# Ternary weights of a fused cross-attention and feed-forward kernel: the 0/1 mask products on TensorE and their PSUM copies replaced by rounding on VectorE, a sign on ScalarE and transposing DMAs

## The reference

```python
x = x + _L0_xattn_ref(_layernorm(x), ctx_1024, ctx_1024, Wq, Wk, Wv, Wo, lam, g)   # 16 heads x 2 softmaxes, d 32, 154 keys
x = x + _L0_ffn_ref(_layernorm(x), ln1_g, ln1_b, w1, b1, ln2_g, ln2_b, w2, b2)

def ternary_quant(w):
    scale = 1.0 / jnp.clip(jnp.mean(jnp.abs(w)), 1e-05)
    wq = jnp.clip(jnp.round(w * scale), -1.0, 1.0) / scale
    return w + jax.lax.stop_gradient(wq - w)

h = layer_norm(x, ln1_g, ln1_b)
h = jnp.einsum('bsd,hd->bsh', h, ternary_quant(w1)) + b1      # w1: 2048 x 512
h = jax.nn.gelu(h, approximate=False)
h = layer_norm(h, ln2_g, ln2_b)
out = jnp.einsum('bsh,dh->bsd', h, ternary_quant(w2)) + b2    # w2: 512 x 2048
```

## Time and profile before

| | us |
|---|---|
| median of 3 runs (2387.71 to 2390.44) | 2389.39 |
| the profiled execution | 2389.21 |
| its span in the profile | 2387.2 |
| busy: PE | 2280.3 |
| busy: DVE | 1673.4 |
| busy: ACT | 1380.1 |
| busy: POOL | 988.1 |

### The profile page before, as it was taken

The page is one execution under the profiler, slowest core; times in us unless marked ns, Lnnn a source line. Parts: engine busy times, 40 slices in busy tenths (PEclk is TensorE's granted clock), DMA queues, the critical chain, the costliest instruction groups (busy, mean ns, idle before and its releaser), DMA issues.

```text
span 2387.2 us, 35788 instructions
## 1 busy us (share of the span) xinstructions
PE 2280.3 (96%) x13791; PEld 1086.3 (46%) x13791; DVE 1673.4 (70%) x2659; ACT 1380.1 (58%) x2001; POOL 988.1 (41%) x807
## 2 busy tenths in 40 slices
PE   8679999999999999999999999999999999999978
PEld 5344535445353544535354454535445453544433
DVE  4677758586776868678686867868676776857663
ACT  3335655566575656657565655656555565665544
POOL 0101625436172534617153452716345271624417
PEclk9779999999999999999999999999999999999989
DMA  7412103030210303021130302112040211202000
GB/s 264 120 29 63 27 24 84 15 88 21 77 33 24 84 15 89 20 67 27 37 86 15 93 15 67 29 50 58 15 108 15 67 28 61 46 24 67 15 23 18
DMA packets 105661, 125.88 MB, mean 53 GB/s; under 512 B 22512, under 2 KB 74284, under 8 KB 104980
## 3 DMA queue, kind: packets, MB, share of 16 engines
q1 hardware_dynamic: 105492, 123.60, 18.5%
HBM read 51.80 MB, written 20.36 MB: 30 GB/s over the span
## 4 chain that ended last, share of the span: by engine, by line
PE 78%; DVE 11%; SPq 4%; ACT 3%; issue 2%; DMA 1%; POOL 1%; POOLq 0%; ACTq 0%; DVEq 0%
PE ps L1443 16%; PE ps L1465 9%; PE ps L1455 9%; PE ps L1286 6%; PE ps L1287 5%; PE ps L1288 5%; PE ps L1341 5%; PE ps L1388 5%; PE ps L1366 4%; PE ps L1395 4%; DVE attn_raw L1013 2%; SPq L456 2%; DVE arena L1074 2%; DVE arena L975 2%; PE ps L1371 2%
## 5 line engine op out<-in xcount | busy, mean ns | idle before, releaser
L566 POOL TENSOR_TENSOR attn_raw<-attn_raw 128x512 f32<-128x512 f32 x448 | 579.3, 1312 | 153.2 <-ACT attn_raw L723 145.9
L1443 PE MATMUL ps<-rows,w1T 128*128 128x512 f16 x2048 | 486.5, 381 | 6.6 <-DVE rows L1069 6.6
L975 DVE TENSOR_REDUCE arena<-ps 128x3 f32<-128x462 f32 (+1 forms) x704 | 412.8, 617 | 105.4 <-PE ps L1341 104.3
L532 POOL TENSOR_TENSOR q<-q 128x512 f16<-128x512 f32 x128 | 152.6, 1198 | 681.1 <-ACT q L669 679.9
L718 ACT ACTIVATE attn_raw<-ps,vec_cols,wstep 128x512 f32<-128x512 f32 x256 | 198.5, 775 | 215.4 <-PE ps L1443 212.9
L1074 DVE SCALAR_TENSOR_TENSOR arena<-attn_raw,vec_cols,arena 128x512 f16<-128x512 f32 x256 | 232.0, 906 | 87.0 <-ACT arena L721 85.2
L1443 PEld LDWEIGHTS ps<-rows,w1T 128*128 128x128 f16 x2048 | 193.6, 98 | 199.7 <-DVE rows L1069 10.8
L1465 PE MATMUL ps<-w2T,arena 128*128 128x512 f16 x1088 | 271.2, 379 | 0.0
L689 ACT ACTIVATE arena<-ps 128x1024 f32<-128x1024 f32 x128 | 131.6, 1028 | 228.3 <-PE ps L1366 228.3
L995 DVE SCALAR_TENSOR_TENSOR p<-arena,p 128x512 f16<-128x512 f32 x128 | 88.1, 688 | 236.7 <-ACT p L693 236.7
L1341 PE MATMUL ps<-k_att,stack_raw 96*128 96x154 f16 x2048 | 221.9, 233 | 27.5 <-DVE arena L975 25.5
(11 more groups left out here) (185 smaller groups left out, 3482.0 us busy)
## 6 DMA issues: line engine op xcount, KB each, us to landing
stack_raw<-q SPq DMA_DIRECT2D x768, 64.0 KB, 2.0
arena<-in_x SPq DMA_DIRECT2D x64, 256.0 KB, 2.6
out<-arena SPq DMA_DIRECT2D x64, 256.0 KB, 2.0
arena<-in_x SPq DMA_DIRECT2D x15, 1024.0 KB, 6.3
arena<-in_L_ffn_w SPq DMA_DIRECT2D x7, 1024.0 KB, 10.0
stack_raw<-in_L_xattn_Wq SPq DMA_DIRECT2D x8, 256.0 KB, 5.8
k_att<-k_store SPq DMA_DIRECT2D x4, 490.0 KB
k_store<-attn_raw SPq DMA_DIRECT2D x12, 160.0 KB
```

The source lines that it names most:

```text
L566: ins = pool.tensor_tensor(acc[:, e, :], acc[:, e, :], src[:, j % NG, :], ALU.add)
L975: dve.tensor_reduce(negmax[:, tt, u0:u1], ps[:, row_bank(c, tb), 0:(u1 - u0) * S].rearrange("p (u s) -> p u s", s=S), AX.X, ALU.max, negat ...
L1443: ins = pe.matmul(ps[:, B_H + j % 2, :], w1T[:, k, j * P:(j + 1) * P], rows16[:, e, k, :], start=(k == 0 and e == 0), stop=(k == KD - 1 an ...
```

## The change

For each of the 32 tiles:

- DVE adds 1.5 x 2^23 to w * scale, in place and in f32, which rounds it to a whole number (one instruction in place of two).
- ACT takes the sign of the result less that number, and writes it in f16 to one of 16 buffers (w1) or 8 (w2): `ternary_sign`, in place of the copy from PSUM. At the ninth tile of w2 it waits until the first eight have been transposed.
- SP issues a DMA that transposes the tile on its way from this buffer to `w1T` or `w2T` (`transpose_ternary`).
- PE's eight matmuls are gone, and with them its waits for masks and copies.

What waited for the copies now waits for the DMAs: the bias product and ACT's first copy of block 0 for all of w1, `h_transposes(0)` for all of w2, and SP itself ahead of `load_x_res(0)`, since those loads overwrite the buffers of w2's signs.

```diff
-PE_PROLOGUE = tokens("x0 q0 q1 a0 q2 t0 t1 t2 q3 t3 t4 t5 q4 t6 t7 m0 q5 t8 t9 m1 q6 t10 m2 t11 q7 m3 t12 m4 t13 m5 t14 "
-                     "m6 t15 m7 m8 m9 m10 b0 x1 n0")
+PE_PROLOGUE = tokens("x0 q0 q1 a0 q2 q3 q4 m0 q5 m1 q6 m2 q7 m3 m4 m5 m6 m7 m8 m9 m10 b0 x1 n0")
+STACKS_AT = {3: 1, 8: 2, 12: 3}
+X_IN1_AT = 6
...
-        signs_late = x_res_raw.bitcast(F16).rearrange("p (n e t) -> p n e t", n=4, e=2)
+        signs_late = x_res_raw.bitcast(F16).rearrange("p (n t) -> p n t", n=8)
...
+            def transpose_ternary(n):
+                dst, landed = ternary_out(n)
+                sp.wait_ge(s_sign, n + 1)
+                sp.dma_start_transpose(dst, sign_tile(n)).then_inc(landed, 16)
...
                 if i == 0:
+                    for n in range(11):
+                        transpose_ternary(JH + n)
                     for p in range(QATT // 2):
                         stack_queries(1, p, 0)
-                    sp.wait_ge(s_ternT, NTERN)
+                    for n in range(11, JH):
+                        transpose_ternary(JH + n)
+                    sp.wait_ge(s_tern[1], 16 * 8)
+                    sp.wait_ge(s_tern[2], 16 * 8)
                     for tt in range(TT):
                         load_x_res(0, tt)
...
-            for p in range(QM // 2):
-                if p == 2:
-                    sp.wait_ge(s_sign, 4)
+            stack_queries(0, 0, None)
+            for n in range(JH):
+                if n in STACKS_AT:
+                    stack_queries(0, STACKS_AT[n], None)
+                if n == X_IN1_AT:
                     load_x_in(1)
-                stack_queries(0, p, None)
+                transpose_ternary(n)
...
-            def ternary_copy(n):
-                act.wait_ge(s_ternT, n + 1)
-                dst, src = ternary_out(n)
-                act.copy(dst, src).then_inc(s_ternC, 1)
+            def ternary_sign(n):
+                src, _ = natural(n)
+                act.wait_ge(s_round, n + 1)
...
+                elif n == JH + 8:
+                    act.wait_ge(s_tern[1], 16 * 8)
+                act.activation(sign_tile(n), src, ACT.Sign, bias=rounder[:, 0:1]).then_inc(s_sign, 1)
...
-                dve.tensor_scalar(pair[:, 0, :], src, wscale[:, w:w + 1], 0.5, ALU.mult, ALU.is_gt)
-                dve.tensor_scalar(pair[:, 1, :], src, wscale[:, w:w + 1], -0.5, ALU.mult, ALU.is_lt).then_inc(s_sign, 1)
+                dve.tensor_scalar(src, src, wscale[:, w:w + 1], ROUNDER, ALU.mult, ALU.add).then_inc(s_round, 1)
...
-                for k in range(KD):
-                    cols = slice(k * P, (k + 1) * P)
-                    pe.matmul(ps[:, bank, cols], pair[:, 0, cols], ident16[:], start=True, stop=False)
-                    ins = pe.matmul(ps[:, bank, cols], pair[:, 1, cols], nident16[:], start=False, stop=True)
-                ins.then_inc(s_ternT, 1)
```

More of the change, by code:

```diff
@@ L87 @@
                "v7 w14 a3 w15")
-SIGNS_AHEAD = 3
+ROUNDED_AHEAD = 3
+ROUNDER = 1.5 * 2.0 ** 23
+STACKS_AT = {3: 1, 8: 2, 12: 3}
+X_IN1_AT = 6
 W1_CUTS, W2_PIECES = (0, 4, 8, 10, 14, 16), 4
@@ L245, in build @@
         negmaxT = sq_acc[0:2 * UNITS, 0:TB // 2].bitcast(F16)
-        signs = attn_raw[:, 0:8 * TB].bitcast(F16).rearrange("p (n e t) -> p n e t", n=8, e=2)
+        signs = attn_raw[:, 0:8 * TB].bitcast(F16).rearrange("p (n t) -> p n t", n=16)
         k16 = attn_raw[:, 0:KV * BATCH * SPAD // 2].bitcast(F16).rearrange(
@@ L369, in natural, with sign_tile @@
             return gg_raw[:, r * HID + q * D:r * HID + (q + 1) * D], 1
-        def sign_pair(n):
-            return signs[:, (n + 4) % 8] if n < JH else signs_late[:, n % 4]
+        def sign_tile(n):
+            return signs[:, (n + 8) % 16] if n < JH else signs_late[:, n % 8]
         block = es.enter_context(nc.Block())
@@ L894, in ternary @@
                 src, w = natural(n)
-                pair = sign_pair(n)
-                if n in (2, 4):
-                    for half in range(2):
-                        dve.wait_ge(s_vst[half], 16 * (n // 2))
-                if 8 <= n < JH:
-                    dve.wait_ge(s_ternT, n - 7)
-                elif n >= JH + 4:
-                    dve.wait_ge(s_ternT, n - 3)
-                dve.tensor_scalar(pair[:, 0, :], src, wscale[:, w:w + 1], 0.5, ALU.mult, ALU.is_gt)
-                dve.tensor_scalar(pair[:, 1, :], src, wscale[:, w:w + 1], -0.5, ALU.mult, ALU.is_lt).then_inc(s_sign, 1)
+                dve.tensor_scalar(src, src, wscale[:, w:w + 1], ROUNDER, ALU.mult, ALU.add).then_inc(s_round, 1)
             def bias_vector():
@@ L1114, in iteration @@
                 if i == 0:
-                    for n in range(SIGNS_AHEAD):
+                    for n in range(ROUNDED_AHEAD):
                         ternary(JH + n)
@@ L1123, in iteration @@
                         attn_lo(i, n)
-                    elif what == "w" and n + SIGNS_AHEAD < JH:
-                        ternary(JH + n + SIGNS_AHEAD)
+                    elif what == "w" and n + ROUNDED_AHEAD < JH:
+                        ternary(JH + n + ROUNDED_AHEAD)
                     elif what == "g" and i:
@@ L1485, in iteration @@
                         scores(i, n)
-                    elif what == "w":
-                        if queries_done > 1:
-                            wait(pe, s_q32, 1, QM, queries_done)
-                        ternary(JH + n)
-                        tiles_done = n + 1
                     elif what == "v":
@@ L1504, in iteration @@
                     elif what == "q" and ahead:
-                        if i == 0 and n:
-                            pe.wait_ge(s_ternC, JH + tiles_done)
                         queries(i + 1, n)
-                        queries_done = n + 1
                 for tt in range(TT):
@@ L1543, in _ @@
             for what, n in PE_PROLOGUE:
-                if what == "t":
-                    ternary(n)
-                elif what == "x":
+                if what == "x":
                     if n:
```

45 lines of the change are left out of this document (21 added, 24 removed).

## The result

| | us |
|---|---|
| kernel before, same chip, median of 9 runs (2387.71 to 2392.47) | 2390.07 |
| changed kernel, median of 9 runs (2392.98 to 2398.53) | 2396.69 |
| ratio, with its 95% interval | 1.0027 [1.0018, 1.0035] |
| profiled execution of the changed kernel | 2396.69 (span 2394.9) |

What follows compares the result with a forecast made beforehand. The prediction took SP's queue order, not TensorE's share, to bound the prologue's end and block 0; prologue 1.8, block 0 5.5 and clock 1.0 us on 2389.21 gave 2397.6, predicted as 2398 us, range 2386 to 2432.

Steps and rivals of the forecast that it cites:

- +8.3: Whole kernel: prologue 1.8, block 0 5.5 and clock 1.0 us added to the profiled execution's 2389.21 us.
- every link of block 0: Transposing DMAs delay residual loads and x on SP's queue; VectorE waits, TensorE idles some 10 us, its clock falls.
- T: Time one transposing DMA holds SP's queue: taken as 1.6 us, range 0.64 to 3.6.
- Prologue, +1.8: Fourth pair of queries starts at 137.8 instead of 136.03 us, behind twelve transposing DMAs; end of prologue 1.8 us later.
- The bound of -4.5 for a small T: Prologue: at most 4.5 us gained, where the last pair waits for its queries again.
- Block 0, +5.5: Residual loads start at 224.2 instead of 218.69 us behind five transposing DMAs; x and the feed-forward half 5.5 us late.
- 3 us off the pairs: Block 0: TensorE's saving ahead of the fourth query product lets the second pair leave SP at 214.8, not 217.8 us.
- The clock, +1: After block 0's stall TensorE's matmuls take twice 0.21 us until 2.4 GHz is granted again: 1 us.
- About 6 us by its last tiles: Block 0: what the attention half gains as a whole by its last tiles, about 6 us.
- The crossbar is the bound: Rival, chance 0.20: T over 2.4 us, ScalarE may stall too in block 0; 2427 us at 3.1, about 2440 at 3.6.
- the transposing DMAs are cheap: Rival, chance 0.20: T up to 0.9 us; prologue gains 4.5, block 0 loses 2.6, clock 1; 2388 us, no change.
- TensorE's time comes back: Rival, chance 0.08: T at most 0.9 us, block 0's attention half returns TensorE's 7.1 and VectorE's 4 us; 2383 us.

Runs made afterwards that it cites:

- run 1: Changed kernel with block 0's load of x for block 2 issued ahead of the last five transposing DMAs; 2391.92 us, 1.0009 of the kernel before.
- run 2: Changed kernel with w2's signs written in place, residual loads at block 0's start and x ahead of the last five transposing DMAs; 2384.19 us, 0.9976.
- Run 3: Changed kernel with four more transposing DMAs, into a spare tile, ahead of the prologue's fourth pair of queries; 2401.02 us, 1.0046 of the kernel before.
- run 5: Changed kernel with the prologue's fourth pair of queries behind ten transposing DMAs instead of twelve; 2395.66 us, 1.0026 of the kernel before.
- run 4: Changed kernel with 44 matmuls of 512 columns added on TensorE in block 0's stall; 2392.10 us, 1.0006 of the kernel before.
- run 8: Changed kernel with 44 matmuls of one column added on TensorE in block 0's stall; 2395.04 us, 1.0021 of the kernel before.
- run 6: run 2 with the prologue's fourth pair of queries behind ten transposing DMAs instead of twelve; 2384.71 us, 0.9979 of the kernel before.
- run 9: run 6 with one 512-column matmul into an unused bank ahead of the wait for w1's last transposing DMA; 2385.31 us, 0.9977.
- run 10: run 6 with 71 filler matmuls of 512 columns in TensorE's waits through the end of the prologue; 2381.73 us, 0.9971 of the kernel before.
- run 7: w1 made as in the changed kernel, w2 by masks, mask products and copies as in the kernel before; 2391.26 us, 1.0005.
- run 11: run 2 with 44 one-column matmuls added on TensorE in the prologue, at its wait for the third pair of queries; 2381.70 us, 0.9972.

## Why the prediction came out

**Forecast 2398, measured 2396.69.** The sum against the profiled execution was +8.3 and came out at +7.5 (2396.69 against 2389.21). Its mechanism was right in every link of block 0, the main one proved by runs 1 and 2. Its terms were less good than the sum, which came so close by luck: the prologue was forecast 2.2 us too high, and the clock and what lies behind the row transposes together 2 us too low (1.0 and 0.9).

**T.** Taken at 1.6, it is 1.30 us, the value of twice a 64 KB DMA, which the prediction had named as the middle. The rows of the key stores, to which I went because a transposition scatters, were the wrong neighbour. The last lands 2.5 us after its issue begins, 1.2 beyond its end, where I took 1.4.

**Prologue, +1.8.** Measured -0.4. With T = 1.30 the prediction's slope (12 us per us of T) gives -1.8. The rest is one transposing DMA of the second group of three that held the queue 1.71 us instead of 1.27 (its sign had been ready for 11 us) and one of the next two that held it 1.52, the gaps of 0.04 to 0.05 us between groups, a load of x of 0.59 instead of 0.52, and a first pair of 8.2 instead of 7.65, less a start 0.3 us sooner. Run 3 confirms the slope; run 5 shows that two DMAs further down it flattens, since w1's own landing ends the wait. The bound of -4.5 for a small T was too generous: the last low half of the queries came at 133.6 instead of 136.0, 2.4 us sooner.

**Block 0, +5.5.** The loads of the residual came 6.6 us later, from two errors that cancel in part. I took 3 us off the pairs that stand ahead. They began 1.3 us sooner (197.70 against 198.98) and ended 0.4 us sooner (217.42 against 217.80), because one of their 24 DMAs held the queue 1.52 us, where before the longest took 0.64 (duration in ns, least, median and most):

```profile
L460 SPq DMA_DIRECT2D stack_raw<-q x24: 586/597/1519, 197.7 to 216.8; - x24
```

Against that, five transposing DMAs took 6.5 instead of 8.0 us. The load of x then was 5.7 us later (227.16), since the four loads ahead of it were issued in 1.78 instead of 2.71 us, and it landed 0.8 us faster (6.70 against 7.5). That makes the +4.84 on VectorE. Its wait was 11.5 us and not about 9, since the attention half had ended 5 us sooner.

**The clock, +1.** This term was sized at half: 2.0 by the trace, 2.3 by runs 4 and 8. I had the mechanism and no row for how long the low clock lasts; it lasted 6 us (236.2 to 242.3), all of them under matmuls.

**Savings.** Mask products: TensorE is busy 8.4 us less in all, where the pace of the starts gave 14.2 (some 3 of the difference are the 15 matmuls that ran at 1.2 GHz behind the stall). "About 6 us by its last tiles" was 5.1, and worth nothing until run 2. The sign costs 0.71 us where I took 0.64 (the activation with a column as scale, 722 ns, was the right neighbour). The Trainium skill has it too, in ScalarE: Activation LUTs, What ACT_TABLE_LOAD costs: 280 ns and 0.833 ns per element with a column as bias. By that it is 707 ns here, an estimate from that page, and the trace agrees (706 ns in the median of w2's signs). VectorE's rounding is 0.48 us as read from the rows scaled in place.

**The rivals.** *The crossbar is the bound* is out, with T far under 2.4, and *the transposing DMAs are cheap* too, with T over 0.9. *TensorE's time comes back* was wrong for this kernel and named the right thing: run 2 gets that result, 2384 where the rival had 2383, not by a cheaper T but by taking the loads from behind the DMAs. I had not seen that the loss was a matter of the order and a buffer alone.

**The Trainium skill's two statements** can now be set beside rows. 32 transposing DMAs of 128 KB add 4.2 MB and, by share times span times the 16 engines, (0.198 x 2394.9) - (0.185 x 2387.2) = 32.6 us of all engines: about 1.02 us each, 129 GB/s (an estimate, with shares rounded to 0.1%). All DMAs of the kernel before, reckoned in the same way, are 123.6 MB in 441.6 us, 280 GB/s. The trace disagrees with Advanced Engine Details and Errata, X-Bar Transpose (TRN2), by which they would be as fast as ordinary DMAs at 350 to 400 GB/s; it disagrees as well with an extrapolation from the 1309 ns for 128 x 128 in VectorE: DVE Perf Modes, The three transpose paths, by which a tile would take 5.2 us (my estimate from it, the page itself gives no rule for more than 128 x 128).

## What to carry to other kernels

Work that is moved from an engine to DMAs is moved into a queue with an order: look up what stands behind it there and who waits for that, before adding up what the engine saves. Here the saving (5 us) was real, the loss (12 us) was one load and one shared buffer behind it, and moving those made the change worth 6 us instead of costing 6.6. TensorE's stall of 10 us cost some 2 us more here than it lasted. An edit that shortens one wait by a microsecond can meet the next one close behind (here w1's own landing). And where single executions differ by some microseconds, one trace of each kernel does not carry a cause for a difference of that size.

## What was not expected of the hardware

- A transposing DMA of 128 x 512 f16, SBUF to SBUF, held SP's queue 1.30 us at its pace back to back (mostly 1.19 to 1.27 by itself, 1.71 and 2.00 at most), landed 2.5 us after issue (5.8 beside the load of x in the prologue), and made 544 packets.
- 44 matmuls of 512 columns in the stall of block 0 kept the clock of 2.4 GHz; 44 of one column did not.
- At the end of the prologue the clock of 2.4 GHz came back either 5 to 7 or 10 to 12 us behind the start of the product that needs all of w1, in traces of the same instructions too (the changed kernel, runs 4 and 8). No run here says why.
- The transposing DMAs disturbed the ordinary ones little: from 130 to 145 us the DMA share was 0.53, before 0.01, 0.26 and 0.44 in the three windows of 5 us, and the last DMA of the fourth pair took 2.07 us to landing instead of 1.99. But among the 24 DMAs of the two pairs in block 0 one held the queue 1.52 us in the changed kernel, and one 0.96 to 1.63 in runs 1 to 6 and 8 to 10; before, and in run 7, which has no transposing DMAs there, none took over 0.64, but in run 11, which has them, none over 0.66. The cause is open.
